# G's products with the weight blocks stationary and w2's 65 columns moving, G transposed afterwards

## The chip, the cores and the metric

The kernel runs on one core of a Trainium2 chip. The metric is the device time of one execution in microseconds (us), lower is better. Engines are called as in the profile: PE is TensorE (matmuls), PEld its weight loads, DVE is VectorE, ACT is ScalarE, POOL is GpSimd, SP is SyncE, which here only issues DMAs.

## The reference, cut to what matters

```python
def tok(idx, wte, w1, b1, w2, b2):       # idx (16, 1024)
    # x[t] = the embeddings (64 wide) of the last 16 tokens, side by side: 1024 columns
    h = tanh(x @ w1 + b1)                # (16, 1024, 64)
    return h @ w2 + b2                   # (16, 1024, 1024)
h = tok(...)
h = h + attn(layernorm(h))               # autocorrelation attention, general case
h = h + ffn(layernorm(h))
def ffn(x, W, bias, A, Bf, coeffs, scales):
    out = x @ W.T + bias
    xa  = einsum('bsd,erd->ebsr', x, A)  # 16 experts of rank 16
    return out + einsum('ebsr,eor,e->bso', xa, Bf, coeffs * scales)
```

Since the token stage is linear in its 64 hidden values (and a constant), the feed-forward part can be applied to w2 once: G = [w2c; b] (W^T + A^T diag(coeffs*scales) Bf), a matrix of 65 rows and 1024 columns, where w2c is w2 (and b2 as row 65) with its mean taken off. Every one of the 128 tiles of output is then a product with 64 rows of w2c and 64 rows of G, scaled and shifted per token, plus a few rank-one rows.

## The kernel before, in words

**Work.** 16 sequences of 1024 tokens, 8 tiles of 128 tokens each. A sequence goes through three stages in a software pipeline, written out by hand as `step(g, u, front, mid, back)`: front (gather the embeddings, transpose them, convolve with w1: `transpose_rows`, `conv_half`, then ACT's tanh), mid (transpose h, moments, variance, the scalings on POOL, split of h into a high and a low part: `transpose_h`, `moments_of`, `transpose_scaled`), back (the output tiles: `even_tile`, `odd_tile`, `four_rank_terms`, and `tile_out` on ACT and DVE). Step k does the front of sequence k, the mid of sequence k-1 and the back of sequence k-2. Every engine works its instructions off in the written order; semaphores tie them together.

**Where G is made.** G must be ready for the back part of step 2. It is built on PE in pieces put between other work: `weight_product(c, halves)` (L1026) for the eight 128-row blocks c of W^T, c = 0 before the steps, 1 to 3 in step 0, 4 to 7 in step 1; then `low_rank_products` (L1071) adds the rank-256 part and sets `g_done`. These are plain fp32 matmuls; the profile shows each as two passes, each with a weight load of its own. Block c of W^T lies in `wT_sb`, which is the memory of `h_all`: POOL's copy of h into `h_all` in step 1 (L454) therefore waits for `g_done`. The 65-column stationary side is `w2cT`, the moving side 512 columns of `wT_sb`; the result is the 65x1024 matrix G in the PSUM banks 0 and 1 of `o_ps`.

**What is done with G, all in step 1.** ACT rounds its 64 rows into `w_hi[64:128]` (L587) and its row 65 into `g_hi` (L588). DVE computes the remainders `w_lo[64:128]` and `g_lo` (`g_lo_halves`, L756 and L758). SP then copies the single rows `g_hi` (twice) and `g_lo` by DMA into `extra` rows 2, 4 and 3 (`row_in`, L319), and copies the eight rows of `extra` to three further partition groups (L351, `rows_in`). `four_rank_terms(0)` of step 2 waits for `rows_in`; the main products of step 2 (L1099) wait for `g_hi_set` and `g_lo_set`, and for the high and low parts of sequence 0 (`hi_kept`, `lo_kept`).

**The order in step 1.** PE: `transpose_rows`, `transpose_h`, product 4, moments, products 5 to 7, low rank, `conv_half(0)`, `transpose_scaled`, `conv_half(1)`. ACT: h parts, G's two copies, `keep_odd(0)` (L541), `take_tanh(0)` (L546), two copies of the scaled h (L610), L612, `keep_odd(1)`, `take_tanh(1)`. DVE: h remainders, `scale_h` (L820 and on, waits for POOL's `beta`), `g_lo_halves`, `add_shifts(0)` (L797), remainders of the scaled h (L907, `lo_kept`), `add_shifts(1)`. `conv_half(1)` waits for `add_shifts(0)`, since both halves use the one bank `conv_ps`.

Of the kernel before, what the change touches and what calls it, by code (L numbers as in the profile page):

```python
# [33 lines left out]
P = 128  # L34
NSEQ, T, L = 16, 1024, 1024
E = 64
# [5 lines left out]
KC = L // P  # L42
# [25 lines left out]
def tower_kernel(nc, ids, wte, w1, b1, w2, b2, wT, bias, aT, bfT, coeffs, scales,  # L68
                 ident, dft, idft, acf, lags, out, force_general=False):
    ctx = ExitStack()  # L70
    with ctx:
# [6 lines left out]
        def sem(name):  # L78
            return ctx.enter_context(nc.semaphore(name))
# [6 lines left out]
        ident_sb = sb("ident_sb", [P, P])  # L86
# [9 lines left out]
        w_hi = sb("w_hi", [P, L], F32R)  # L96
# [5 lines left out]
        bfT_sb = sb("bfT_sb", [P, 2, L])  # L102
# [38 lines left out]
        obuf = sb("obuf", [P, 4, 2, L])  # L141
# [14 lines left out]
        wT_sb = h_all[:, :].rearrange("p (c n) -> p c n", c=KC)  # L156
        w1_ld = obuf[:, 0, 0, :].rearrange("p (j n) -> p j n", j=J)
        w2cT = obuf[:, 0, 1, 0:KC * (E + 1)].rearrange("p (c n) -> p c n", c=KC)
        xa_sb = obuf[0:E + 1, 1, 0, 0:ER]
        xaT_sb = obuf[:, 1, 0, ER:ER + 2 * (E + 1)].rearrange("p (c n) -> p c n", c=2)  # L160
        er_ld = obuf[:, 1, 0, 512:516]
        xbar_rows = xT[0][0:KC, 0:P]

        b_hi, b_lo = w_hi[E:E + 1, :], w_lo[E:E + 1, :]
        bias_hi, bias_lo = u_hi[1][0:1, :], u_lo[1][0:1, :]
        g_hi, g_lo = u_hi[1][96:97, :], u_lo[1][96:97, :]
# [12 lines left out]
        o_ps = ps("o_ps", [P, 4, 512])  # L179
# [13 lines left out]
        def y_view(hh):  # L193

            return (mix_ps, sum_ps)[hh][:, 0:4 * (E + 3)].rearrange("p (j two n) -> p j two n", j=2, two=2)

        def in_pairs(rows):

# [28 lines left out]
        mom_kept = sem("mom_kept")  # L227
# [2 lines left out]
        xa_done = sem("xa_done")  # L230
        xa_kept = sem("xa_kept")
        g_done = sem("g_done")
        base_hi_set = sem("base_hi_set")
        base_lo_set = sem("base_lo_set")
        g_hi_set = sem("g_hi_set")
        g_lo_set = sem("g_lo_set")
        row0_in, rows_in = sem("row0_in"), sem("rows_in")
# [53 lines left out]
        def in_step(k, g, u):  # L291

            return isinstance(g, int) and 2 * g + u == k
# [190 lines left out]
        def _(act):  # L484
# [36 lines left out]
            def step(g, u, front, mid, back):  # L521
                a, b, c = 2 * g + u, 2 * g + u - 1, 2 * (g - 1) + u
# [13 lines left out]
                def keep_odd(hh):  # L536

                    act.wait_ge(conv_done, 2 * a + hh + 1)
                    ge(act, shifts_added, 2 * a + hh)
                    n = HALF - hh  # L540
                    nc.scalar.copy(odd[0:E, HALF * hh + 1:HALF * hh + 1 + n], conv_ps[E:P, 0:n]).then_inc(odd_kept, 1)  # L541
# [40 lines left out]
                    keep_h_hi(1)  # L582
                    keep_h_hi(2)
                if in_step(1, g, u):
                    act.wait_ge(row0_in, 16 * 5)
                    act.wait_ge(g_done, 1)
                    nc.scalar.copy(w_hi[E:P, :], o_ps[0:E, 0:2, :].rearrange("p a n -> p (a n)")).then_inc(g_hi_set, 1)  # L587
                    nc.scalar.copy(g_hi, o_ps[E:E + 1, 0:2, :].rearrange("p a n -> p (a n)")).then_inc(g_hi_set, 1)  # L588
                if front:
                    keep_odd(0)  # L590
                if mid and not front:
                    keep_h_hi(0)
                if back:
# [63 lines left out]
        def _(dve):  # L657
# [88 lines left out]
                nc.vector.tensor_tensor(w_lo[0:E + 1, :], w2c[:, :], w_hi[0:E + 1, :].bitcast(F32), ALU.subtract).then_inc(base_lo_set, 1)  # L746
                nc.vector.tensor_tensor(bias_lo, bias_row[:, :], bias_hi.bitcast(F32), ALU.subtract).then_inc(base_lo_set, 1)

            gw = o_ps[0:E, 0:2, :].rearrange("p a n -> p (a n)")
            gb = o_ps[E:E + 1, 0:2, :].rearrange("p a n -> p (a n)")  # L750

            def g_lo_halves():

                dve.wait_ge(row0_in, 16 * 5)
                dve.wait_ge(g_hi_set, 1)
                nc.vector.tensor_tensor(w_lo[E:P, :], gw, w_hi[E:P, :].bitcast(F32), ALU.subtract).then_inc(g_lo_set, 1)  # L756
                dve.wait_ge(g_hi_set, 2)
                nc.vector.tensor_tensor(g_lo, gb, g_hi.bitcast(F32), ALU.subtract).then_inc(g_lo_set, 1)  # L758
# [15 lines left out]
            def step(g, u, front, mid, back):  # L774
                a, b, c = 2 * g + u, 2 * g + u - 1, 2 * (g - 1) + u
# [18 lines left out]
                def add_shifts(hh):  # L794
                    dve.wait_ge(odd_kept, 2 * a + hh + 1)
                    cols = slice(HALF * hh, HALF * (hh + 1))
                    nc.vector.tensor_tensor(hT[u][E * hh:E * hh + E, 0:HALF], conv_ps[0:E, :], odd[0:E, cols],  # L797
                                            ALU.add).then_inc(shifts_added, 1)
# [82 lines left out]
                    keep_h_lo(1)  # L881
                if in_step(1, g, u):
                    scale_h()
                    g_lo_halves()
                if front:
                    add_shifts(0)
                if back:
                    tile_out(c, u, 4)
                if not front and not mid:
# [38 lines left out]
            with dve.If(need != 0):  # L928
# [6 lines left out]
                with dve.Fori(0, NSEQ * NT) as t:  # L935
# [67 lines left out]
                    for n in range(2):  # L1003
                        last = nc.vector.tensor_scalar(spec_w[:, P * n:P * (n + 1)], sum_ps[:, P * n:P * (n + 1)],
                                                       er_w[:, n:n + 1], None, ALU.mult)
# [9 lines left out]
        def _(pe):  # L1015
            mm, tr = nc.tensor.matmul, nc.tensor.transpose
# [4 lines left out]
            for c in range(KC):  # L1021
                bank = (sum_ps, mix_ps)[c // 4]
                last = tr(bank[:, (E + 1) * (c % 4):(E + 1) * (c % 4 + 1)], w2c[:, P * c:P * (c + 1)], ident_sb[0:E + 1, 0:E + 1])
            last.then_inc(w2T_done, 1)

            def weight_product(c, halves):  # L1026

                if c % 2 == 0:
                    pe.wait_ge(wT_in[c // 2], 16)
                for n in halves:  # L1030
                    mm(o_ps[0:E + 1, n, :], w2cT[:, c, :], wT_sb[:, c, 512 * n:512 * (n + 1)], start=(c == 0), stop=False)

            def xa_product(first, end):

# [6 lines left out]
            for c in range(KC):  # L1041
                last = mm(o_ps[0:E + 1, 2, 0:E + 1], w2cT[:, c, :], w2cT[:, c, :], start=(c == 0), stop=(c == KC - 1))
# [28 lines left out]
            def low_rank_products():  # L1071
                pe.wait_ge(bfT_in, 16)
                for e in range(2):
                    for n in range(2):
                        last = mm(o_ps[0:E + 1, n, :], xaT_sb[:, e, :], bfT_sb[:, e, 512 * n:512 * (n + 1)], start=False, stop=(e == 1))
                last.then_inc(g_done, 1)

            def xbar_correlation():

# [9 lines left out]
            def step(g, u, front, mid, back):  # L1089
                a, b, c = 2 * g + u, 2 * g + u - 1, 2 * (g - 1) + u  # L1090
# [43 lines left out]
                def transpose_scaled():  # L1134

                    pe.wait_ge(u_ready, b + 1)
                    for j in range(NT // 2):
                        last = tr(sum_ps[:, P * j:P * (j + 1)], bh_row[:, 2 * j:2 * j + 2, :].rearrange("p i e -> p (i e)"),  # L1138
                                  ident_sb[:, :])
                    last.then_inc(ut_done, 1)  # L1140
                    pe.wait_ge(x_ready, b + 1)
                    ge(pe, et_lo_kept, 2 * (a + front))
                    for q in range(NT // 2):
                        last = tr(et_ps[:, P * q:P * (q + 1)],  # L1144
                                  x_row[:, 2 * q:2 * q + 2, :, :].bitcast(F32).rearrange("p i d x -> p (i d x)"), ident_sb[:, :])
                    last.then_inc(xt_done, 1)
# [32 lines left out]
                def conv_half(hh):  # L1179

                    if in_step(0, g, u) and hh == 0:
                        pe.wait_ge(shift_set, 2)
                        pe.wait_ge(pads_set, 2)
                        pe.wait_ge(pad_conv_kept, 1)
                    if hh == 0:
                        pe.wait_ge(et_lo_kept, 2 * a + 2)
                    ge(pe, shifts_added, 2 * a + hh)
                    col = PAD + HALF * hh
                    for m in range(J // 2):
                        mm(conv_ps[:, :], shift_hi[:, 2 * m:2 * m + 2, :], et_hl[u][:, col - 2 * m:col - 2 * m + HALF],  # L1190
                           start=(m == 0), stop=False)
                    if hh == 0:
                        pe.wait_ge(et_top_kept, a + 1)
                        pe.wait_ge(et_back_kept, a + 1)
                    for m in range(J // 4):
                        last = mm(conv_ps[:, :], shift_lo[:, 2 * m:2 * m + 2, :], et_hh[u][:, col - 2 * m:col - 2 * m + HALF],  # L1196
                                  start=False, stop=(m == J // 4 - 1))
                    last.then_inc(conv_done, 1)
# [12 lines left out]
                if in_step(1, g, u):  # L1211
                    transpose_rows()
                    transpose_h()
                    weight_product(4, (0, 1))
                    moments_of(0)
                    moments_of(1)
                    for k in range(5, KC):
                        weight_product(k, (0, 1))
                    low_rank_products()
                    conv_half(0)  # L1220
                    transpose_scaled()
                    conv_half(1)
                    return
# [66 lines left out]
            with pe.If(need != 0):  # L1290
# [26 lines left out]
                with pe.Fori(0, NSEQ * NT) as t:  # L1317
# [30 lines left out]
                    for e in range(2):  # L1348
                        for c in range(KC):
                            last = mm(sum_ps[:, P * e:P * (e + 1)], aT_sb[:, c, P * e:P * (e + 1)], ab1[:, P * c:P * (c + 1)],  # L1350
                                      start=(c == 0), stop=(c == KC - 1))
# [53 lines left out]
```

## Time and profile before

| | |
|---|---|
| runs | 399.44, 400.08, 402.02 us; median 400.08 |
| profiled execution | 399.41 us, its span on the core 397.5 us |
| busy | PE 96%, DVE 70%, ACT 62%, POOL 54% |
| chain that ended last | PE 84%, POOL 6%, engines waiting for nothing shown 4%, DVE 2%, DMA 2% |
| granted TensorE clock | 0.996 in the mean |
| instructions | 6799 |

The span is the time from the first to the last instruction; the profiled execution's own time is 1.9 us longer. All times below are microseconds from the start of the span. Matmuls are pipelined: their records overlap, so the time that one costs is read from start to start of the ones in a row, not from its own duration.

### The profile page before, as it was taken

How to read it: one execution, taken by the hardware profiler on the slowest of the kernel's cores; microseconds unless marked ns; L12 is line 12 of the kernel's file. 1: busy time of each engine (PE TensorE's matmuls, PEld its weight loads, DVE VectorE, ACT ScalarE, POOL GpSimd, SP SyncE). 2: the span in 40 equal slices, each digit the busy share in tenths (PEclk: the TensorE clock that was granted, in tenths of full speed). 3: DMA queues.
4: the chain of work that ended last, by engine and by line, in shares of the span. 5: the costliest groups of instructions: out<-in, count | busy, mean ns of one | idle time of the engine just before them, and what ended most of it. 6: DMA issues, size and time to landing. Idle time of an engine off the chain costs nothing.

```text
span 397.5 us, 6799 instructions
## 1 busy us (share of the span) xinstructions
PE 380.2 (96%) x1908; PEld 276.5 (70%) x1908; DVE 276.3 (70%) x602; ACT 246.3 (62%) x362; POOL 214.7 (54%) x284
## 2 busy tenths in 40 slices
PE   1998999999999999999999999999999999999993
PEld 1554567777778777777777777777777777777662
DVE  2855567686868777786868687777868696876752
ACT  2524465766667666757666676667576666765642
POOL 6745748475574748374665747473846654312200
PEclk9999999999999999999999999999999999999998
DMA  9793045545545555555455455555554654445475
GB/s 213 216 353 112 12 130 213 187 192 206 209 174 211 192 221 224 211 202 207 172 212 223 157 208 205 221 224 202 200 215 166 223 213 155 203 195 240 194 307 215
DMA packets 28692, 79.86 MB, mean 201 GB/s; under 512 B 7194, under 2 KB 8490, under 8 KB 28676
## 3 DMA queue, kind: packets, MB, share of 16 engines
q1 hardware_dynamic: 23968, 75.19, 48.2%
q0 software_dynamic: 4096, 4.20, 5.3%
q10 hardware_dynamic: 612, 0.27, 0.4%
q8 instruction: 8, 0.13, 0.2%
q14 instruction: 8, 0.07, 0.0%
HBM read 12.40 MB, written 67.12 MB: 200 GB/s over the span
## 4 chain that ended last, share of the span: by engine, by line
PE 84%; POOL 6%; issue 4%; DVE 2%; DMA 2%; SPq 0%; POOLq 0%; DVEq 0%
PE o_ps L1099 46%; PE conv_ps L1190 13%; PE o_ps L1125 7%; PE conv_ps L1196 7%; POOL gathered L405 5%; PE sum_ps L1164 2%; PE sum_ps L1176 2%; PE mix_ps L1176 2%; PE sum_ps L1138 2%; PE et_ps L1144 2%; PE et_ps L1154 2%; DMA extra<-extra 1%; DVE obuf L718 1%; DMA ids_sb<-in_ids 1%; POOL inv_std L440 1%
## 5 line engine op out<-in xcount | busy, mean ns | idle before, releaser
L405 POOL DMA_INDIRECT gathered<-in_wte,idx_now x128 | 128.0, 1000 | 44.1 <-issue 34.3
L518 ACT ACTIVATE obuf<-o_ps,mean_sb,a_sb 128x512 f32<-128x512 f32 x128 | 99.7, 779 | 75.4 <-PE o_ps L1125 47.2
L718 DVE TENSOR_SCALAR obuf<-o_ps,a_sb,mean_sb 128x512 f32<-128x512 f32 x128 | 102.4, 809 | 58.5 <-PE o_ps L1099 33.0
L1099 PE MATMUL o_ps<-w_hi,u_hi 128*128 128x512 f32 x256 | 110.3, 431 | 0.0
L1099 PE MATMUL o_ps<-w_hi,u_lo 128*128 128x512 f32 x256 | 101.2, 395 | 0.0
L1099 PE MATMUL o_ps<-w_lo,u_hi 128*128 128x512 f32 x256 | 101.1, 395 | 0.0
L1190 PE MATMUL conv_ps<-et_hl,shift_hi 128*128 128x512 f32 x256 | 65.4, 397 | 0.8 <-DVE hT L797 0.8
L1099 PEld LDWEIGHTS o_ps<-w_hi,u_hi 128*128 128x128 f32 x256 | 48.1, 188 | 21.5 <-issue 12.6
L1190 PEld LDWEIGHTS conv_ps<-et_hl,shift_hi 128*128 128x128 f32 x256 | 48.1, 188 | 13.5 <-DVE hT L797 1.6
L1099 PEld LDWEIGHTS o_ps<-w_lo,u_hi 128*128 128x128 f32 x256 | 48.1, 188 | 11.6
L1099 PEld LDWEIGHTS o_ps<-w_hi,u_lo 128*128 128x128 f32 x256 | 48.3, 189 | 6.7
L436 POOL TENSOR_SCALAR var_eps<-var 128x8 f32<-128x8 f32 x16 | 3.2, 198 | 87.8 <-DVE var L847 87.8
L541 ACT COPY odd<-conv_ps 64x512 f32<-64x512 f32 (+1 forms) x32 | 18.7, 584 | 38.7 <-PE conv_ps L1196 38.7
L797 DVE TENSOR_TENSOR hT<-conv_ps,odd 64x512 f32<-64x512 f32 x32 | 21.9, 683 | 26.1 <-ACT odd L541 25.7
L1196 PE MATMUL conv_ps<-et_hh,shift_lo 128*128 128x512 f32 x128 | 35.0, 395 | 0.0
L1125 PE MATMUL o_ps<-extra,xT 8*128 8x512 f32 x256 | 32.3, 495 | 0.7 <-DMA extra<-extra 0.6
L440 POOL TENSOR_TENSOR inv_std<-var_eps,minus_half 128x8 f32<-128x8 f32 x16 | 27.9, 1746 | 2.3 <-POOL var_eps L436 1.8
L1125 PEld LDWEIGHTS o_ps<-extra,xT 8*128 8x128 f32 x256 | 12.3, 181 | 24.3 <-issue 23.3
L450 POOL TENSOR_TENSOR beta<-var_eps,minus_half 128x8 f32<-128x8 f32 x16 | 26.9, 1682 | 2.3 <-POOL var_eps L448 1.8
L1196 PEld LDWEIGHTS conv_ps<-et_hh,shift_lo 128*128 128x128 f32 x128 | 24.1, 189 | 5.6
L546 ACT ACTIVATE hT<-hT,b_col 64x512 f32<-64x512 f32 x32 | 22.9, 716 | 3.6 <-DVE hT L797 3.3
L787 DVE TENSOR_TENSOR et_hl<-et_ps,et_hl 64x512 fp32r<-64x512 f32 x32 | 22.1, 689 | 3.6 <-ACT et_hl L528 2.7
(133 smaller groups left out, 440.7 us busy)
## 6 DMA issues: line engine op xcount, KB each, us to landing
out<-obuf SPq DMA_DIRECT2D x127, 512.0 KB, 2.8
h_all<-in_wT SPq DMA_DIRECT2D x4, 1024.0 KB, 6.5
gathered<-in_wte,idx_now POOLq DMA_INDIRECT x128, 2.9
aT_sb<-in_aT SPq DMA_DIRECT2D x1, 1024.0 KB
bfT_sb<-in_bfT SPq DMA_DIRECT2D x1, 1024.0 KB, 12.2
obuf<-in_w SPq DMA_DIRECT2D x2, 256.0 KB, 7.3
lagged<-xbar_twice SPq DMA_DIRECT2D x1, 512.0 KB, 3.7
out<-obuf SPq DMA_DIRECT2D x2, 256.0 KB, 3.0
```

Source lines behind the costliest of these rows:

```text
L405: pool.indirect_dma_start(gathered[p][:, i, :], None, wte, bass.IndirectOffsetOnAxis(ap=idx_now[p][:, i:i + 1].bitcast(U32), axis=0),).the ...
L440: pool.tensor_tensor(inv_std[:, :], var_eps[:, :], minus_half[:, :], ALU.pow).then_inc(scal_step, 1)
L450: pool.tensor_tensor(beta[:, :], var2_eps[:, :], minus_half[:, :], ALU.pow).then_inc(scal_step, 1)
L518: nc.scalar.activation(obuf[:, q, i % 2, 0:512], o_ps[:, 2 * (i % 2), :], ACT.Identity, bias=mean_sb[pc][:, i:i + 1], scale=a_sb[pc][:, i: ...
L546: nc.scalar.activation(hT[u][rows, 0:HALF], hT[u][rows, 0:HALF], ACT.Tanh, bias=b1_col[rows, 0:1]).then_inc(tanh_done, 1)
L718: nc.vector.tensor_scalar(obuf[:, q, i % 2, 512:L], o_ps[:, 2 * (i % 2) + 1, :], a_sb[pc][:, i:i + 1], mean_sb[pc][:, i:i + 1], ALU.mult, ...
L787: nc.vector.tensor_tensor(lo, pair_bank(et_ps, odd_tiles), hi.bitcast(F32), ALU.subtract).then_inc(et_lo_kept, 1)
L797: nc.vector.tensor_tensor(hT[u][E * hh:E * hh + E, 0:HALF], conv_ps[0:E, :], odd[0:E, cols], ALU.add).then_inc(shifts_added, 1)
L1099: last = mm(o_ps[:, 2 * (i % 2) + n, :], lhsT, rhs[:, 512 * n:512 * (n + 1)], start=(i % 2 == 0 and f == 0), stop=(i % 2 == 1 and f == len ...
L1125: ins = mm(o_ps[:, k, :], xT[u][rows, P * q:P * (q + 1)], extra[rows, 512 * (k % 2):512 * (k % 2 + 1)], start=(k >= 2), stop=(k < 2))
L1190: mm(conv_ps[:, :], shift_hi[:, 2 * m:2 * m + 2, :], et_hl[u][:, col - 2 * m:col - 2 * m + HALF], start=(m == 0), stop=False)
L1196: last = mm(conv_ps[:, :], shift_lo[:, 2 * m:2 * m + 2, :], et_hh[u][:, col - 2 * m:col - 2 * m + HALF], start=False, stop=(m == J // 4 - 1))
```

## The change

The two sides of G's products change places. The stationary side is now a 128x128 block of `wT_sb` (or `bfT_sb`), the moving side `w2cT` (or `xaT_sb`) with its 65 columns: eight matmuls per block row c where there were two, ten block rows in all. The result is G transposed, in eight pieces of 128x65, four to a bank (`gT_bank`). ACT copies both banks to `gT_sb`; PE turns the eight pieces back (`turn_g`, after `conv_half(0)`) into the banks 2 and 3 of `o_ps`; ACT's and DVE's work on G reads them there. On ACT this work moves behind `keep_odd(0)`, on DVE `g_lo_halves` moves behind `add_shifts(0)`.

```diff
 # weight_product(c, halves), PE
-                for n in halves:
-                    mm(o_ps[0:E + 1, n, :], w2cT[:, c, :], wT_sb[:, c, 512 * n:512 * (n + 1)], start=(c == 0), stop=False)
+                for half in halves:
+                    for n in range(KC // 2):
+                        col = P * (KC // 2 * half + n)
+                        mm(gT_bank(half)[:, n, :], wT_sb[:, c, col:col + P], w2cT[:, c, :], start=(c == 0 and n == 0), stop=False)
 # low_rank_products, PE
-                    for n in range(2):
-                        last = mm(o_ps[0:E + 1, n, :], xaT_sb[:, e, :], bfT_sb[:, e, 512 * n:512 * (n + 1)], start=False, stop=(e == 1))
+                    for n in range(KC):
+                        last = mm(gT_bank(n // 4)[:, n % 4, :], bfT_sb[:, e, P * n:P * (n + 1)], xaT_sb[:, e, :], start=False, stop=(e == 1 and n % 4 == 3))
                 last.then_inc(g_done, 1)
+            def turn_g():
+                pe.wait_ge(gT_kept, 2)
+                pe.wait_ge(mom_kept, 5)
+                for n in range(KC):
+                    last = tr(o_ps[0:E + 1, 2 + n // 4, P * (n % 4):P * (n % 4 + 1)], gT_sb[:, n, :], ident_sb[:, :])
+                last.then_inc(g_turned, 1)
 # step 1, PE
                     low_rank_products()
                     conv_half(0)
+                    turn_g()
                     transpose_scaled()
                     conv_half(1)
 # step 1, ACT
                 if in_step(1, g, u):
-                    act.wait_ge(row0_in, 16 * 5)
                     act.wait_ge(g_done, 1)
-                    nc.scalar.copy(w_hi[E:P, :], o_ps[0:E, 0:2, :].rearrange("p a n -> p (a n)")).then_inc(g_hi_set, 1)
-                    nc.scalar.copy(g_hi, o_ps[E:E + 1, 0:2, :].rearrange("p a n -> p (a n)")).then_inc(g_hi_set, 1)
+                    for half in range(2):
+                        nc.scalar.copy(gT_sb[:, 4 * half:4 * half + 4, :], gT_bank(half)).then_inc(gT_kept, 1)
                 if front:
                     keep_odd(0)
+                if in_step(1, g, u):
+                    act.wait_ge(row0_in, 16 * 5)
+                    act.wait_ge(g_turned, 1)
+                    nc.scalar.copy(w_hi[E:P, :], o_ps[0:E, 2:4, :].rearrange("p a n -> p (a n)")).then_inc(g_hi_set, 1)
+                    nc.scalar.copy(g_hi, o_ps[E:E + 1, 2:4, :].rearrange("p a n -> p (a n)")).then_inc(g_hi_set, 1)
 # step 1, DVE
                 if in_step(1, g, u):
                     scale_h()
-                    g_lo_halves()
                 if front:
                     add_shifts(0)
+                if in_step(1, g, u):
+                    g_lo_halves()
```

## Rows read from the trace of the kernel before

**Rows 1.** Windows: start:end and length; PE, PEld, DVE, ACT, POOL busy; PEclk; DMA
```profile
54.00:385.00 331.00, 330.98 (x1700) 247.32 (x1699) 243.15 (x525) 221.63 (x327) 179.61 (x235) 1.00 0.53 205
...
391.40:394.50 3.10, 0.00 (x0) 0.00 (x0) 0.59 (x1) 0.56 (x1) 0.00 (x0) 1.00 0.86 329
394.60:397.50 2.90, 0.00 (x0) 0.00 (x0) 0.00 (x0) 0.00 (x0) 0.00 (x0) 0.50 0.04 12
```

**Rows 2.** The chain in order of time, 0 to 80: start, length, what
```profile
42.87 0.69 DVE u_rows L820
...
44.50 1.22 DVE w_lo L756
...
45.75 1.24 DVE u_lo L758
...
47.00 1.76 DMA extra<-u_lo
...
52.96 0.51 PE o_ps L1125 x4
```

**Rows 3.** PE's timeline, 28 to 51: start, length of the group, what
```profile
30.99 0.66 PE L1154 MATMUL et_ps<-ident_sb,gathered 128*128 128x128 f32 x4 [1.19 <-DMA gathered<-in_wte,idx_now]
...
34.55 5.31 PE L1031 MATMUL o_ps<-h_all,obuf 128*65 128x512 f32 x12
39.70 3.60 PE L1075 MATMUL o_ps<-bfT_sb,obuf 128*65 128x512 f32 x8
...
45.91 0.60 PE L1138 MATMUL sum_ps<-ident_sb,u_rows 128*128 128x128 f32 x4
46.35 0.60 PE L1144 MATMUL et_ps<-ident_sb,x_row 128*128 128x128 f32 x4
47.74 2.12 PE L1190 MATMUL conv_ps<-et_hl,shift_hi 128*128 128x512 f32 x8 [0.79 <-DVE hT L797]
...
50.74 0.47 PE L1099 MATMUL o_ps<-w_hi,u_hi 128*128 128x512 f32 x1
```

**Rows 4.** Timelines of PE and PEld: short fp32 operations before 35
```profile
33.64 0.62 PE L1176 MATMUL mix_ps<-moments_two,hT 128*128 128x134 f32 x4
34.09 0.62 PE L1176 MATMUL sum_ps<-moments_two,hT 128*128 128x134 f32 x4
...
13.71 0.29 PEld L1052 LDWEIGHTS o_ps<-moments,hbar 1*128 1x128 f32 x2
...
27.79 0.28 PE L1068 MATMUL mix_ps<-ident_sb,obuf 65*128 65x65 f32 x2
```

**Rows 5.** One line's instructions: durations ns min/median/max
```profile
L1176 PEld LDWEIGHTS mix_ps<-moments_two,hT x64: 190/190/192, 33.2 to 359.1; 128*128 128x128 f32 x64
...
L1052 PEld LDWEIGHTS o_ps<-moments,hbar x2: 181/182/184, 13.7 to 13.8; 1*128 1x128 f32 x2
...
L1068 PE MATMUL mix_ps<-ident_sb,obuf x2: 221/222/223, 27.8 to 27.9; 65*128 65x65 f32 x2
...
L1031 PE MATMUL o_ps<-h_all,obuf x32: 591/592/1057, 11.1 to 39.3; 128*65 128x512 f32 x32
```

**Rows 6.** ACT's timeline
```profile
8.84 0.37 ACT L498 COPY obuf<-mix_ps 128x260 f32<-128x260 f32 x1
...
43.39 1.01 ACT L587 CAST w_hi<-o_ps 64x1024 fp32r<-64x1024 f32 x1 [6.92 <-PE o_ps L1075]
...
46.11 0.58 ACT L541 COPY odd<-conv_ps 64x512 f32<-64x512 f32 x1 [0.69 <-PE conv_ps L1196]
...
48.47 1.19 ACT L610 CAST u_hi<-sum_ps 64x512 fp32r<-64x512 f32 x2
```

**Rows 7.** DVE's and POOL's timelines
```profile
47.01 0.68 DVE L797 TENSOR_TENSOR hT<-conv_ps,odd 64x512 f32<-64x512 f32 x1
49.08 1.41 DVE L907 TENSOR_TENSOR u_lo<-sum_ps,u_hi 64x512 fp32r<-64x512 f32 x2 [1.39 <-ACT u_hi L610]
...
37.38 0.20 POOL L436 TENSOR_SCALAR var_eps<-var 128x8 f32<-128x8 f32 x1
```

More of the change, by code:

```diff
@@ L162, in tower_kernel @@
         xbar_rows = xT[0][0:KC, 0:P]
+        gT_sb = obuf[:, 2, 0, 0:KC * (E + 1)].rearrange("p (n e) -> p n e", n=KC)
         b_hi, b_lo = w_hi[E:E + 1, :], w_lo[E:E + 1, :]
@@ L195, in y_view, with gT_bank @@
             return (mix_ps, sum_ps)[hh][:, 0:4 * (E + 3)].rearrange("p (j two n) -> p j two n", j=2, two=2)
+        def gT_bank(half):
+            return o_ps[:, half, 0:KC // 2 * (E + 1)].rearrange("p (n e) -> p n e", e=E + 1)
         def in_pairs(rows):
@@ L232, in tower_kernel @@
         g_done = sem("g_done")
+        gT_kept = sem("gT_kept")
+        g_turned = sem("g_turned")
         base_hi_set = sem("base_hi_set")
@@ L747, in base_lo_halves @@
                 nc.vector.tensor_tensor(bias_lo, bias_row[:, :], bias_hi.bitcast(F32), ALU.subtract).then_inc(base_lo_set, 1)
-            gw = o_ps[0:E, 0:2, :].rearrange("p a n -> p (a n)")
-            gb = o_ps[E:E + 1, 0:2, :].rearrange("p a n -> p (a n)")
+            gw = o_ps[0:E, 2:4, :].rearrange("p a n -> p (a n)")
+            gb = o_ps[E:E + 1, 2:4, :].rearrange("p a n -> p (a n)")
             def g_lo_halves():
```

## The prediction

> **What bounds the kernel now.** I read the windows first: from 54 to 385 PE is busy 330.98 of 331.00 us [rows 1]. Nothing behind the start-up has room, so whatever PE gains or loses before 54 shifts the rest rigidly. The change only touches what comes before, so the next views are the chain in order of time and the timelines up to 54. The chain leaves `scale_h` (DVE, 42.87) for the two remainders of G (44.50 and 45.75, done at 46.99), the DMA of row `g_lo` (47.00), the copies of `extra`, and reaches PE's `four_rank_terms(0)` at 52.96 [rows 2]. From then on PE never stops. So the question is one date: when do G's rows reach `extra`? PE's own stream before it is nearly as tight: an idle 1.19 in front of 30.99 (gathered rows, from POOL) and 0.79 in front of 47.74 (`add_shifts(0)`, which DVE starts at 47.01 behind G's remainders) [rows 3, 7].
>
> **The products themselves.** Before, a pass of 512 columns costs (39.70 - 34.55)/12 = 0.429 us [rows 3]; a block row is 4 passes, 1.72. After, it is 8 matmuls of 2 passes, 16 passes with a 128-column weight load and 65 moving columns. The trace has no such pass, so I bound it. The moving side alone: `xa_by_columns` streams 65 columns, its two passes start 0.28 - 0.22 = 0.06 us apart [rows 4, 5]. The load alone: two 128-column fp32 loads in front of 3-column matmuls start 0.29 - 0.18 = 0.108 apart, so they are the limit there [rows 4, 5]. Do load and stream add up? In the moments each pass has a 128-column load of 190 ns and streams 134 columns, and passes start (34.09 - 33.64)/4 = 0.113 apart [rows 4, 5]: the load lies wholly beside the stream before it. So the pass costs the larger of the two, 0.109 (the load, nearest row 0.108; 0.113 at the upper end). The ends for the range are 0.060 and 0.108 + 0.060 = 0.168. A block row is then 16 x 0.109 = 1.74 against 1.72: **nothing is gained**, since the halved stream makes the doubled load the limit.
>
> The Trainium skill says the opposite of overlap: in "TensorE: Matmul & The Clock Gate", the section "Measured speedup vs the span model", a weight load overlaps a running matmul only where the row group differs, and here all 128 rows are used. By that rule the pass would be the sum of both; the moments' rows contradict it, and I give it a small chance below.
>
> Products 0 to 3 lie before 30.99: 64 passes, at most 0.3 us more, under the 1.19 us that PE waits there for gathered rows; without that cover they would cost 0.3. Product 4 and the two 0.11 passes of the moments do not move POOL: its `var_eps` at 37.38 starts with no idle before it, behind a gather [rows 7]. After 30.99 come six block rows: 96 x 0.109 - 24 x 0.429 = +0.15 us. `g_done` gates POOL's copy into `h_all` and five gathers, all +0.15, and sequence 2's rows are needed after `four_rank_terms(0)`, which moves more.
>
> **The way of G after them.** Before, ACT's copy into `w_hi` starts at 43.39 right behind the products and ends at 44.40, just as DVE leaves `scale_h` (0.69 from 42.87, then small ones to about 44.43), and the remainders start at 44.50 [rows 2, 6]. After:
> - ACT copies the two banks, 0.37 each [rows 6], from about 43.5 to 44.2, in time it waited away before; PE is in `conv_half(0)`. Cost nothing; without that cover 0.7.
> - `conv_half(0)` ends at 45.91 [rows 3] + 0.15 = 46.06. `turn_g` is 8 fp32 transposes at (46.35 - 45.91)/4 = 0.11 [rows 3] = 0.87: to 46.93, result at about 47.10 (a transpose group's record of 0.60 is 0.16 longer than its 0.44 of starts).
> - ACT has ended `keep_odd(0)` (0.58 from 46.11 + 0.15) at 46.84 and waits for `g_turned`: `w_hi` 47.19 to 48.20, `g_hi` to 49.2 (1.01 each) [rows 6]. SP's two DMAs of `g_hi` follow at once, beside DVE's work.
> - DVE has added shifts at 46.9 to 47.6, in the gap. The remainders start at 48.24 instead of 44.50 and end after the same 2.49 at 50.73. The last row's DMA starts at 50.74, and the rest, the row, SP's three copies and their landing, takes 52.96 - 47.00 = 5.96 as before [rows 2]: **56.70 instead of 52.96, +3.74 us**.
>
> Beside it: PE's `transpose_scaled` moves to 46.93 to 47.80; `conv_half(1)` starts at 47.8 without its wait of 0.79, thus when it did before (47.74). The 0.87 of `turn_g` is paid by that idle time. Queued behind ACT's later copies are `take_tanh(0)` and L610: L610 (before at 48.47) now starts at 49.2 + 0.75 = 49.9, so DVE's L907, 1.41 from 49.08, now runs from about 50.7 behind the remainders to 52.1 [rows 6, 7]. The main products of `even_tile(0)`, before at 50.74 [rows 3], wait for it until 52.15, are six passes of 512 columns, at about 0.24 each 1.4 (the eight of L1190 span 2.12 with their tail [rows 3]), and end at 53.55. That wait of 1.4 is inside the longer one: PE then stands 3.15 until 56.70. `keep_odd(1)`, `add_shifts(1)`, `take_tanh(1)` end near 53.8 and are needed at 57. Sum: 399.41 (profiled) + 3.74 = 403.15; against the median 400.08, 0.67 above the profiled one, 403.8. I say 403.7.
>
> **The rivals.**
> - *The clock falls in the new gap.* PE would stand 1.4, work 1.4, stand 3.15. After the last matmul of the trace PE does nothing from 391.40; the granted clock is 1.00 to 394.50 and 0.50 after 394.60 [rows 1]: 3.1 us of nothing were survived there, a bit more was not. Idle stretches of 1.2 cost nothing. If it falls to 1.2 GHz, the first pass of 512 columns in the trace shows what that means: 1057 ns against 592 [rows 5]. How long it would stay low no row says (at the start it was low up to that pass at 11.1); if about as long as the gap, 3 us of work run at half speed and cost 1.5 more: 405.2. For: the gap is as long as the one survived. Against: work of 1.4 us in front.
> - *Load and stream add up* (by the skill's rule above): 0.168 per pass, 96 x 0.059 = 5.7 more after 30.99, and 64 x 0.059 = 3.8 before less the cover of 1.19, 2.6: 412. The point from which it decides is any pass above 0.12. Against it stand the moments.
> - *Not slower: the load is hidden better than its row says*, pass 0.060. Then `g_done` comes 96 x 0.049 = 4.7 earlier. But `scale_h` still waits for POOL's `beta` and ends at 44.43; the new order puts `add_shifts(0)` (0.68 [rows 7]) in front, so the remainders start at 45.15 instead of 44.50: +0.65, 400.7. Below a pass of about 0.077 this limit holds, and no pass makes the time better than before. For: only that loads of half the width took 0.06; against: the 0.108.
> - *Faster by over 1%* needs G's rows at 49, which neither `scale_h` nor the 5.96 of DMAs permits; I leave it for what I may have overlooked.
>
> **How the numbers follow.** A measurement of this kernel tells some 1%, 4 us, from no change. Forecast (+3.7, from +3.2 to +4.9 with a pass of 0.113 and the noise of the runs): 0.70. Clock: 0.10. Adding up: 0.06. Short passes: 0.11. Faster: 0.03. The range 402.0 to 406.0 holds the forecast and the clock case, 0.80. The limit of 1% is at 404.08, just above the forecast: a quarter to a third of its 0.70 lies beyond (0.22), with clock 0.10 and adding 0.06, 0.38 slower; 0.59 within 1%; 0.03 faster. The sign is surer than that: an increase has 0.95.
>
> **What would show it.** The new products at 0.109 from start to start, `g_done` near 43.5; `turn_g` at 46.1; the `w_hi` copy at 47.2; the remainders at 48.2; PE idle before the main products of step 2 and about 3 us before the first L1125 group at 56.7, then none; clock 1.00 throughout. Products at 0.06, or an L1125 group before 55, would make it wrong, as would later idle time on PE that absorbs the shift.

## The result, and the profile after

The changed kernel takes 406.57 us (median of 4, 405.43 to 406.83) against 399.76 (median of 4, 399.06 to 402.02): ratio 1.0164, 95% interval 1.0138 to 1.019, **6.8 us slower**. The forecast was 403.7, range 402.0 to 406.0: right in sign, too small, outside the range. The profiled execution took 406.65, its span is 404.8, 7.3 longer than before.

PE's timeline after, from the first products to step 2; columns as in [rows 3]. L1057 is the first product of w2c with itself, which starts the stretch; L1052 are the products with A^T (aT below), L1177 the transposes of gathered rows, L1046 are G's products, L1090 the low-rank ones, L1098 `turn_g`, L1148 `four_rank_terms`:

```profile
9.35 2.02 PE L1057 MATMUL o_ps<-obuf 128*65 128x65 f32 x16 [1.20 <-ACT obuf L506]
...
11.16 1.92 PE L1046 MATMUL o_ps<-obuf,h_all 128*128 128x65 f32 x8
12.88 0.32 PE L1063 MATMUL o_ps<-hbar,moments 65*65 65x1 f32 x2
...
15.94 3.56 PE L1052 MATMUL sum_ps<-aT_sb,obuf 128*65 128x256 f32 x8
...
19.63 0.66 PE L1177 MATMUL et_ps<-ident_sb,gathered 128*128 128x128 f32 x4
20.12 1.89 PE L1052 MATMUL sum_ps<-aT_sb,obuf 128*65 128x256 f32 x8
...
32.98 0.60 PE L1177 MATMUL et_ps<-ident_sb,gathered 128*128 128x128 f32 x4
...
36.58 5.47 PE L1046 MATMUL o_ps<-obuf,h_all 128*128 128x65 f32 x48
41.88 3.74 PE L1090 MATMUL o_ps<-obuf,bfT_sb 128*128 128x65 f32 x32
45.43 2.10 PE L1213 MATMUL conv_ps<-et_hl,shift_hi 128*128 128x512 f32 x8
47.36 1.09 PE L1219 MATMUL conv_ps<-et_hh,shift_lo 128*128 128x512 f32 x4
48.30 1.04 PE L1098 MATMUL o_ps<-ident_sb,obuf 128*65 128x128 f32 x8
...
54.73 0.47 PE L1122 MATMUL o_ps<-w_hi,u_hi 128*128 128x512 f32 x1 [1.74 <-DVE u_lo L920]
...
58.67 0.51 PE L1148 MATMUL o_ps<-extra,xT 8*128 8x512 f32 x4 [2.29 <-DMA extra<-extra]
```

The same stretch of the kernel before, ahead of [rows 3]; L1042, L1037 and L1154 there are L1057, L1052 and L1177 here:

```profile
9.26 2.02 PE L1042 MATMUL o_ps<-obuf 128*65 128x65 f32 x16 [1.23 <-ACT obuf L498]
...
14.38 1.94 PE L1037 MATMUL sum_ps<-aT_sb,obuf 128*65 128x256 f32 x8
...
16.46 0.66 PE L1154 MATMUL et_ps<-ident_sb,gathered 128*128 128x128 f32 x4
```

Three things are to be seen, against these and [rows 2, 3]:
- The new products cost what was forecast: (41.88 - 36.58)/48 = 0.110 us a pass.
- But PE is late before any of it matters. The first group of L1052 takes 3.56, the second, eight passes too, 1.89: TensorE is still at its lower level of 1.2 GHz at 16 us. (The windows of this profile print a granted clock of 1.00 for this stretch too; at the start of a profile the level is therefore read from the durations.) Before, the first such group already took 1.94: the higher level, 2.4 GHz. So a group is slow that the change doesn't touch. PE reaches the gathered rows of sequence 0 at 19.63 instead of 16.46 and those of sequence 1 at 32.98 instead of 30.99, without waiting for them: the cover of 1.19 is used up and 1.99 is lost.
- From `turn_g` on the forecast's distances hold within 0.3 (48.30 to L1148 is 10.37; forecast 46.06 to 56.70, 10.64), with both predicted idle stretches (1.74 and 2.29; forecast 1.4 and 3.15). Between 32.98 and 48.30 PE loses 0.40 where the forecast had 0.15, so two small misses cancel.

The windows of the same profile (columns as in [rows 1]) show the rest:

```profile
36.60:45.40 8.80, 8.80 (x82) 8.80 (x80) 5.50 (x21) 1.77 (x3) 5.61 (x8) 1.00 0.05 10
...
56.38:58.66 2.28, 0.00 (x1) 0.00 (x0) 0.00 (x0) 0.00 (x0) 0.14 (x1) 1.00 0.26 45
...
60.30:63.60 3.30, 3.30 (x12) 2.72 (x11) 1.12 (x5) 1.43 (x4) 0.00 (x0) 0.50 0.39 159
63.70:400.00 336.30, 334.50 (x1711) 248.77 (x1710) 246.01 (x530) 222.60 (x327) 179.24 (x234) 1.00 0.54 207
```

After the two idle stretches the granted clock is 0.50 from 60.3 to 63.7, with PE busy all the time: the work of 1.7 us at 2.4 GHz is done there in 3.4. So 7.3 = 5.71 (L1148 at 58.67 instead of 52.96) + 1.6, and 5.71 = 3.74 forecast + 1.97.

G's way on ACT, and then on DVE, in the timelines of the changed kernel, the rows that answer [rows 2, 6, 7]:

```profile
49.43 1.01 ACT L601 CAST w_hi<-o_ps 64x1024 fp32r<-64x1024 f32 x1 [0.35 <-PE o_ps L1098]
```
```profile
49.11 0.68 DVE L809 TENSOR_TENSOR hT<-conv_ps,odd 64x512 f32<-64x512 f32 x1 [3.82 <-ACT odd L549]
50.53 1.22 DVE L768 TENSOR_TENSOR w_lo<-o_ps,w_hi 64x1024 fp32r<-64x1024 f32 x1 [0.74 <-ACT w_hi L601]
51.78 1.22 DVE L770 TENSOR_TENSOR u_lo<-o_ps,u_hi 1x1024 fp32r<-1x1024 f32 x1
53.04 1.41 DVE L920 TENSOR_TENSOR u_lo<-sum_ps,u_hi 64x512 fp32r<-64x512 f32 x2
```

`add_shifts(0)` (L809) stands first, `w_hi` starts 1.13 after `turn_g`, the remainders follow it, and `lo_kept` (L920) comes last at 54.45, which PE's main products wait for: each in the order and at the distances of the forecast.

### The profile page after: what moved, and what is told of

It is laid out like the page before. It is cut to its first block, busy times and chain, and to the rows that moved or that the text cites. A ratio compares the mean times of both kernels' runs of the same rounds, so it can differ in the third digit from the quotient of the medians.

```text
span 404.8 us, 7058 instructions
## 1 busy us (share of the span) xinstructions
PE 385.9 (95%) x2036; PEld 293.5 (73%) x2036; DVE 276.0 (68%) x602; ACT 246.9 (61%) x364; POOL 213.4 (53%) x284
## 4 chain that ended last, share of the span: by engine, by line
PE 93%; DMA 2%; DVE 2%; ACT 0%; ACTq 0%; SPq 0%; issue 0%; DVEq 0%
PE o_ps L1122 46%; PE conv_ps L1213 14%; PE conv_ps L1219 7%; PE o_ps L1148 7%; PE o_ps L1046 4%; PE sum_ps L1187 2%; PE sum_ps L1199 2%; PE mix_ps L1199 2%; PE et_ps L1177 2%; PE sum_ps L1161 2%; PE et_ps L1167 2%; DMA b_col<-in_b 1%; PE sum_ps L1052 1%; PE o_ps L1090 1%; DMA extra<-extra 1%; DVE obuf L730 1%
## 5 line engine op out<-in xcount | busy, mean ns | idle before, releaser
L809 DVE TENSOR_TENSOR hT<-conv_ps,odd 64x512 f32<-64x512 f32 x32 | 21.9, 683 | 29.5 <-ACT odd L549 29.0
L1148 PE MATMUL o_ps<-extra,xT 8*128 8x512 f32 x256 | 32.2, 495 | 2.4 <-DMA extra<-extra 2.3
L1148 PEld LDWEIGHTS o_ps<-extra,xT 8*128 8x128 f32 x256 | 12.3, 181 | 26.0 <-issue 23.2
## 6 DMA issues: line engine op xcount, KB each, us to landing
bfT_sb<-in_bfT SPq DMA_DIRECT2D x1, 1024.0 KB, 12.9
```

What stands on the lines that cost most here:

```text
L1148: ins = mm(o_ps[:, k, :], xT[u][rows, P * q:P * (q + 1)], extra[rows, 512 * (k % 2):512 * (k % 2 + 1)], start=(k >= 2), stop=(k < 2))
```

## The experiments

**Two ways to take the clock out.** Theory: 3.7 us are G's longer way, 2.0 the late rise of the clock, the rest its fall in the gap. Rival: the form of the products, or a fourth cause, costs 2 us or more at full clock too. Warm-up:

```diff
+            pe.wait_ge(warm_set, 1)          # DVE has set hT[0] to 1.0
+            for n in range(3):
+                mm(conv_ps[:, :], hT[0][:, 0:P], hT[0][:, 0:HALF], start=True, stop=True)
             pe.wait_ge(consts_in, 16)
 ...
             last.then_inc(w2T_done, 1)
+            mm(conv_ps[:, :], hT[0][:, 0:P], hT[0][:, 0:HALF], start=True, stop=True)
```

Fill (7 before the main products' wait, 9 before `rows_in`):

```diff
+                for n in range(7):           # and 9 before pe.wait_ge(rows_in, 48)
+                    mm(mix_ps[:, :], shift_hi[:, 0:2, :], et_hl[1][:, PAD:PAD + HALF], start=True, stop=True)
```

> The kernel before, with four extra fp32 matmuls of 512 columns on a constant tile (three before PE's first transposes, one between them and the first products), so that TensorE works from about 1.5 us on. Clock theory (start-up level matters only where PE is late): the granted clock is up before 9 us, products 0 start at the higher level, but the kernel before waits 1.19 us for gathered rows at 30.99 anyway, so L1125 still starts within 0.3 of 52.96 and the time is 399.8 give or take 0.6. Rival (the start-up's PE time is on the path in the kernel before too): 1 us or more faster.

Measured 399.07 (10 runs, 398.6 to 401.31) against 399.48: ratio 1.0002 (0.9982 to 1.0021). The clock theory holds for the time, but not by the wait that was expected. PE's timeline:

```profile
14.44 1.94 PE L1043 MATMUL sum_ps<-aT_sb,obuf 128*65 128x256 f32 x8 [1.28 <-DMA aT_sb<-in_aT]
...
29.67 0.60 PE L1160 MATMUL et_ps<-ident_sb,gathered 128*128 128x128 f32 x4
...
47.47 2.12 PE L1196 MATMUL conv_ps<-et_hl,shift_hi 128*128 128x512 f32 x8 [1.81 <-DVE hT L799]
```

The gathered rows are there at 29.67 in this execution, and PE doesn't wait for them: the cover of 1.19 is not the same in every execution. PE is done with `transpose_scaled` early and waits 1.81 instead of 0.79 for `add_shifts(0)`; L1131 starts at 52.71.

> The changed kernel with the same four extra matmuls. Clock theory: of the 5.7 us by which G's rows came late, 2.0 come from TensorE being at the lower level until 19.3; with it up by 9 us the products before 31 us are done in time, PE waits for gathered rows again, turn_g starts near 46.1 and the first L1148 group near 56.7, and the time is 403.5 (405.2 if the clock falls again in the gap after). Rival (the products themselves or something else of the change is dearer by 2 us before 33 us, at full clock too): turn_g stays at 48.3 and L1148 at 58.7, time 405.0 to 406.6.

Measured 404.73 (4 runs, 403.55 to 405.37): ratio 1.0135 (1.0114 to 1.0157), between the two theories. The profile is of the fastest of the four, 403.55; the others have mean granted clocks of 0.987 to 0.991 against its 0.991. PE's timeline, warm-up in front (L1036), then the windows:

```profile
1.45 4.58 PE L1036 MATMUL conv_ps<-hT 128*128 128x512 f32 x6 [1.45 <-DVE hT L671]
...
9.27 1.16 PE L1063 MATMUL o_ps<-obuf 128*65 128x65 f32 x16 [0.58 <-ACT obuf L507]
10.26 1.06 PE L1052 MATMUL o_ps<-obuf,h_all 128*128 128x65 f32 x8
12.32 0.28 PE L1069 MATMUL o_ps<-hbar,moments 65*65 65x1 f32 x2 [1.00 <-DVE moments L694]
...
17.42 1.11 PE L1183 MATMUL et_ps<-ident_sb,gathered 128*128 128x128 f32 x4
...
57.05 0.51 PE L1154 MATMUL o_ps<-extra,xT 8*128 8x512 f32 x4 [2.32 <-DMA extra<-extra]
```
```profile
8.50:11.90 3.40, 2.24 (x25) 1.92 (x24) 1.21 (x8) 1.95 (x5) 2.68 (x3) 1.00 1.21 241
12.00:15.30 3.30, 2.87 (x20) 2.37 (x21) 2.77 (x10) 1.60 (x2) 2.42 (x5) 0.99 0.58 178
15.40:18.70 3.30, 3.30 (x12) 2.02 (x11) 2.09 (x4) 0.28 (x2) 2.69 (x3) 0.51 0.80 248
```

The clock was up, and **fell again** from 15.4 to 18.6, behind block 0 of the new products, an idle 1.00 in the middle of it and the small matmuls after it. In the kernel before with the same warm-up it did not, over the same stretch and with an idle 1.28 in it. So in this profile the warm start didn't last through the new block 0, and this run can't isolate the 2.0. L1154 came at 57.05, and no fall followed although PE stood 1.71 and 2.32 before it.

> The changed kernel with 7 and 9 extra fp32r matmuls of 512 columns in PE's two idle stretches of step 2 (before the main products wait, and before L1148 waits for the copied rows), writing a free bank. Clock theory: no fall of the clock at 60.3; L1148 still at 58.7 or as late as the start-up makes it; PE without idle time from then; 405.0, that is 1.5 less than the changed kernel in the runs in which its clock fell and the same in the others. Rival (the clock's fall costs nothing that PE has not lost already): no change, 406.5.

Measured 405.69 (405.52 to 408.57): ratio 1.0178 (1.0138 to 1.0218). No fall in the profile: PE is back at 58.98 and the span is 403.6, 1.2 under the profiled changed kernel's 404.8. The medians (405.69 and 406.57) don't separate it from the changed kernel.

> Both of these in the changed kernel. Clock theory: only the forecast's term is left, the later way of G's rows: L1148 near 56.7, no low clock from 9 us to the end of PE's work, 3.7 above the kernel before, 403.5. Rival (there is a fourth cause): above 404.5.

Measured 405.39, from 402.21 to 406.97: inconclusive. Its four runs have mean granted clocks of 0.989, 0.998, 0.993 and 0.983, and their times are in that order: 402.21 at 0.998, 406.97 at 0.983. In the profile the clock was low from 12.9 to 19.6.

**Block 0 alone, both ways round.** Since the warm-up couldn't hold the clock, the form of block 0 itself was changed.

```diff
 # old0_after: in the changed kernel, G's first block left out
+                    if c == 0:
+                        mm(o_ps[0:E + 1, half, :], w2cT[:, c, :], wT_sb[:, c, 512 * half:512 * (half + 1)], start=True, stop=True)
+                        continue
 # new0_before: in the kernel before, G's first block left out
+                    if c == 0:
+                        for n in range(KC // 2):
+                            col = P * (KC // 2 * half + n)
+                            mm(o_ps[:, half, (E + 1) * n:(E + 1) * (n + 1)], wT_sb[:, c, col:col + P], w2cT[:, c, :],
+                               start=(n == 0), stop=(n == 3))
+                        continue
```

> The changed kernel with block 0 of the products (the two halves before the steps) in the old form, G's first block left out of the sum. Form theory (at the lower clock level the new form, loads with a half as long stream behind each, does not bring the clock up as the old one does): the clock rises near 12 to 16 instead of 19 to 20, PE reaches 19.6 some 2 to 3 us earlier, turn_g near 46.2, L1148 near 56.8, time 403.7 (1.6 more if the clock falls in the gap). Rival (the late rise is chance of the executions, or comes from anything else in the start-up): rise at 19 to 20, L1148 at 58.7, 405.5 to 406.6.

Measured 403.55 (403.0 to 404.32): ratio 1.0096 (1.0073 to 1.012). The form theory holds. The profile is of the slowest of the four.

```profile
9.57 2.02 PE L1060 MATMUL o_ps<-obuf 128*65 128x65 f32 x16 [1.17 <-ACT obuf L506]
...
14.73 1.89 PE L1055 MATMUL sum_ps<-aT_sb,obuf 128*65 128x256 f32 x8
...
16.93 0.66 PE L1180 MATMUL et_ps<-ident_sb,gathered 128*128 128x128 f32 x4
...
56.24 0.51 PE L1151 MATMUL o_ps<-extra,xT 8*128 8x512 f32 x4 [2.61 <-DMA extra<-extra]
```

This is PE's timeline. The first aT group (L1055) takes 1.89, thus at the higher level, and PE is at the gathered rows of sequence 0 at 16.93. Seven blocks and the low-rank part in the new form, the turn and the order cost 56.24 - 52.96 = 3.3 here. In the median 3.0 of the 6.8 us go with block 0's new form.

> The reverse: the kernel before with block 0 of the products in the new form (its result overwritten by block 1, so G lacks its first block). Form theory: clock up at 19 to 20 instead of 12.25, PE 3 us later at 20, 1.2 of it absorbed in front of the gathered rows at 31, the rest on G's way: L1125 near 54.8, time 401.5. Rival: unchanged, 399.5.

Measured 403.33 (402.49 to 404.9): ratio 1.0089 (1.0065 to 1.0112), more than expected. Of the profile, PE's timeline:

```profile
12.29 2.02 PE L1049 MATMUL o_ps<-obuf 128*65 128x65 f32 x16 [4.46 <-ACT obuf L498]
...
18.88 3.62 PE L1044 MATMUL sum_ps<-aT_sb,obuf 128*65 128x256 f32 x8
...
22.72 1.11 PE L1161 MATMUL et_ps<-ident_sb,gathered 128*128 128x128 f32 x4
```

Here the first product also started 3 us late, at 12.29, behind ACT; that differs from execution to execution (9.2 to 9.7 in ten of the profiles, 11.3 to 12.4 in four). What ACT waits for is the DMA of b1. Its timeline here, and then in the kernel before:

```profile
11.39 0.31 ACT L495 ACTIVATE hbar<-b_col 64x128 f32<-64x128 f32 x1 [3.37 <-DMA b_col<-in_b]
```
```profile
8.37 0.31 ACT L495 ACTIVATE hbar<-b_col 64x128 f32<-64x128 f32 x1 [1.69 <-DMA b_col<-in_b]
```

This tanh of b1 stands ahead of ACT's copies of the transposed w2 (L498), and it starts at 10.4 to 11.6 in the four late profiles, at 8.3 to 8.8 in the ten others. The form's share is therefore read from the first product to the gathered rows' transposes: 22.72 - 12.29 = 10.43, against 16.46 - 9.26 = 7.2 in the kernel before. All profiles fall in two groups: block 0 old 7.1, 7.2, 7.2 (one of them warmed), 7.4, 7.7, 8.1 and 8.3; block 0 new and not warmed 10.3, 10.4, 10.4, 10.4 and, with 16 columns in the later blocks, 10.0. That is 1.7 to 3.3 us for block 0 alone. (Warmed, the new form has 8.2 and 9.0.) Why the other three runs, at 402.49 to 403.61, also lie above the expected 401.5 is not shown.

**The order and the turn.**

```diff
 # order_before: in the kernel before
+                if front:
+                    keep_odd(0)              # ACT: now ahead of G's two copies
                     act.wait_ge(g_done, 1)
 ...
                     scale_h()
-                    g_lo_halves()
                 if front:
                     add_shifts(0)
+                if in_step(1, g, u):
+                    g_lo_halves()
```

> The kernel before with only the changed kernel's order: ACT rounds G behind keep_odd(0), DVE takes G's remainders behind add_shifts(0). Products, their form and their place stay, nothing is transposed. Order theory (most of the forecast's 3.74 is the order, not the transposes): ACT's w_hi at 46.75, remainders from 47.8 instead of 44.5, L1125 at 56.2, 3.3 more than before: 402.8, and up to 1.7 more where the clock falls in PE's gap. Rival (the turn behind conv_half(0) is what costs): 1 us at most, 400.5.

Measured 404.13 (403.64 to 407.46): ratio 1.0122 (1.01 to 1.0145). With no product and no transpose changed, the order alone costs 4.7 us in the median. Its profile started late (11.36), so the distance is read, on PE's timeline, from the end of `conv_half(0)` (start of L1139, or of `turn_g` in the changed kernel) to `four_rank_terms(0)`:

```profile
47.57 0.60 PE L1139 MATMUL sum_ps<-ident_sb,u_rows 128*128 128x128 f32 x4
...
53.65 0.47 PE L1100 MATMUL o_ps<-w_hi,u_hi 128*128 128x512 f32 x1 [1.49 <-DVE u_lo L908]
...
57.99 0.80 PE L1126 MATMUL o_ps<-extra,xT 8*128 8x512 f32 x4 [2.69 <-DMA extra<-extra]
```

10.42 here, 58.67 - 48.30 = 10.37 in the changed kernel, 52.96 - 45.91 = 7.05 in the kernel before [rows 2, 3]: the order alone brings the whole 3.3, and the turn, which runs beside `keep_odd(0)`, adds nothing to it. The window behind the gap:

```profile
57.80:64.50 6.70, 6.51 (x25) 5.49 (x26) 2.15 (x6) 2.85 (x5) 0.00 (x0) 0.50 0.19 78
```

Gaps of the same size (1.49 and 2.69) are followed by a fall of the clock here too, and for 6.8 us, with the products in the old form: the fall doesn't need the new products. Of the four profiles with unfilled gaps three show it (this one, the changed kernel, old0_after), warm_after doesn't; of the three with filled gaps none does. So the gap makes a fall there possible, not certain. This profile is of the slowest of five runs; four of the five have mean clocks of 0.988 to 0.991, so much of the 1.3 us over the expected 402.8 may be such falls; late starts are the other candidate.

> The changed kernel with turn_g right behind the low-rank products, and ACT's and DVE's work on G before keep_odd(0) and add_shifts(0), as in the kernel before. With a start-up as late as the changed kernel's: products end at 45.4, turn at 46.3 to 47.2, remainders from 48.4 instead of 50.5, L1148 near 56.7 instead of 58.7, PE's gap before it near 1 us instead of 2.3, so no fall of the clock there: 403.5. If the way of G were not what sets L1148: 406.5.

```diff
                     low_rank_products()
+                    turn_g()
                     conv_half(0)
-                    turn_g()
 # and on ACT and DVE G's work stands before keep_odd(0) and add_shifts(0) again
```

Measured 404.4 (403.61 to 405.68): ratio 1.0133 (1.0106 to 1.016), 2.2 under the changed kernel. L1147 starts at 57.09 with 0.38 idle instead of 2.29 and no fall follows, though the first aT group is as late (3.62) as in the changed kernel. As expected but for 0.9 in the median.

Both edits, this one and old0_after's, in one kernel:

> The changed kernel with both repairs: block 0 in the old form (left out of the sum) and turn_g right behind the low-rank products with ACT's and DVE's old order. If the two causes add: clock up by 12 to 16, turn_g at 43.7, remainders from 45.8, L1148 near 54.2, 401.1, that is 1.2 us above the kernel before, the way through the copy and the transposes alone. If they don't add (another wait takes over): 402.5 or more.

Measured 401.59 (6 runs, 400.54 to 404.44): ratio 1.0047 (1.002 to 1.0074). The causes add: the two edits alone took 3.0 and 2.2 off 406.57, together 5.0. Its profile is of the slowest run, which started late (12.44), and in which the clock was low from 46.4 to 49.7, behind the new products and the 0.74 that PE waits for ACT's copy of G transposed.

And the fill in old0_after:

> The changed kernel with block 0 in the old form and the 16 extra matmuls in PE's two gaps of step 2. Clock theory: no low clock from 16 us to the end of PE's work; only the forecast's term is left: L1150 near 56.4, 3.6 above the kernel before, 403.1, and never the 1.5 that the clock's fall added in one profile of the kernel without the fill. Rival: same times as without the fill, falls included.

Measured 403.39 (402.93 to 404.56): ratio 1.0106 (1.0082 to 1.0131). In the profile the clock holds, L1153 is at 56.44 and the execution took 402.95: the forecast's term without clock effects, 403.1 expected. Against old0_after's 403.55 the medians show no difference. Its profiled run, the slowest of four at 404.32, has a mean clock of 0.991 and the low stretch; the others have 0.994 and 0.995, which suggests that they didn't have it.

**The limit of a pass.**

> The changed kernel with 16 moving columns instead of 65 in blocks 1 to 7 and the low-rank products (G's other columns left out). If the 128-column weight load is the limit of a pass: passes start 0.108 to 0.111 us apart as with 65 columns. If load and stream add: 0.07 to 0.12 less than with 65, if the stream were the limit: 0.03. A second question: whether the clock holds in the 8.8 us of such products from 36 us on, which it did with 65 columns; a fall there would double them to 0.215.

```diff
-                        mm(gT_bank(half)[:, n, :], wT_sb[:, c, col:col + P], w2cT[:, c, :], ...)
+                        w = E + 1 if c == 0 else WM          # WM = 16
+                        mm(gT_bank(half)[:, n, 0:w], wT_sb[:, c, col:col + P], w2cT[:, c, 0:w], ...)
```

One run, 414.96. PE's timeline and the windows of its step 1:

```profile
33.93 1.86 PE L1048 MATMUL o_ps<-obuf,h_all 128*128 128x16 f32 x16
35.64 0.70 PE L1201 MATMUL mix_ps<-moments_two,hT 128*128 128x134 f32 x4
...
36.63 7.67 PE L1048 MATMUL o_ps<-obuf,h_all 128*128 128x16 f32 x48
44.14 6.99 PE L1092 MATMUL o_ps<-obuf,bfT_sb 128*128 128x16 f32 x32
```
```profile
36.60:39.40 2.80, 2.80 (x28) 2.80 (x26) 2.73 (x12) 1.83 (x3) 1.21 (x3) 1.00 0.11 26
39.50:56.50 17.00, 17.00 (x69) 15.74 (x70) 2.72 (x10) 0.68 (x3) 8.34 (x11) 0.50 0.03 7
```

A pass with 16 columns costs (35.64 - 33.93)/16 = 0.107, with 65 it costs 0.110: the stream is not the limit, and load and stream do not add up. That it is the load, and not a fixed cost of each pass, the first lines of warm_after show: there L1063 streams 65 columns behind loads of 65, at the higher level, and its passes start (10.26 - 9.27)/16 = 0.062 apart. And the clock falls at 39.5 in the middle of the 16-column products, with PE and PEld busy without a break; with 65 columns it held through 8.8 us of them. Why it fell is open, and so is whether it would in another execution: this is one run.

**A version faster than both.** [Rows 2] put `g_lo` last on the way to `extra`. It needs only G's row 65, so that row goes first:

```diff
-                    nc.scalar.copy(w_hi[E:P, :], o_ps[0:E, 0:2, :]...).then_inc(g_hi_set, 1)
                     nc.scalar.copy(g_hi, o_ps[E:E + 1, 0:2, :]...).then_inc(g_hi_set, 1)
+                    nc.scalar.copy(w_hi[E:P, :], o_ps[0:E, 0:2, :]...).then_inc(g_hi_set, 1)
 # the same on DVE; SP waits for g_hi_set 1 and g_lo_set 1
```

> The kernel before with G's row 65 taken before its 64 rows on ACT and DVE, so that the DMAs into extra start 1.25 us earlier, at 45.75. If the rows' way alone sets L1125: it starts at 52.4, right behind the main products, 0.6 us earlier, and the time is 398.9 against 399.5. If PE's stream is as late anyway: no change.

Measured 398.8 (12 runs, 398.62 to 399.94) against 399.44 (19 runs): ratio 0.9984 (0.9973 to 0.9995), as expected: 0.6 us, small, but the interval excludes 1. PE's timeline:

```profile
52.16 0.51 PE L1125 MATMUL o_ps<-extra,xT 8*128 8x512 f32 x4
```

The idle 0.59 in front of L1125 is gone; PE stands 0.21 behind it instead, for ACT's tanh.

## Why the prediction was wrong

- **The products, 0.109 us a pass: right.** 0.110 measured, and the 16-column run, with the 0.062 of 65-column loads, shows the load as the limit. The rule of the Trainium skill that I weighed, that a load overlaps a running matmul only where the row group differs, stands in "TensorE: Matmul & The Clock Gate" in the section "The mechanism", not where I placed it. The runs contradict it for this case: 0.110 a pass, not 0.168, so a full-row load lies beside the matmul before it. They fit another sentence of that section, by which a load into the background weight buffer is pulled ahead too. Two slips didn't matter: 96 x 0.109 - 24 x 0.429 is 0.17, not 0.15, and the two passes of `xa_by_columns`, 0.06 apart, have loads of 128 columns and 65 rows (L1068), not of half the width; they are transposes, whose loads have records of 140 ns against the moments' 190, so their 0.06 bounds no plain product's load.
- **G's way, +3.74: right.** Without the start-up's share L1151 stands at 56.24 and L1153 at 56.44 (forecast 56.70), the times are 403.55 and 403.39 (forecast 403.7). The telling was incomplete: I spoke of `turn_g` and its result at 47.1, but `order_before` shows that the order alone brings as much (10.42 against 10.37 from the end of `conv_half(0)`), while early_after, with the old order, takes 1.8 more than the kernel before from the start of the low-rank products to `four_rank_terms(0)` (57.09 - 42.06 against 52.96 - 39.70): the copy and the transposes are not free where the order doesn't hide them. `add_shifts(0)` waits for `keep_odd(0)` and thus for all of `conv_half(0)`; whatever DVE has behind it can't start before 47.4.
- **The failed step: "Products 0 to 3 lie before 30.99: 64 passes, at most 0.3 us more, under the 1.19 us that PE waits there for gathered rows."** It priced all of them at the higher clock level, and put what block 0 does to the level behind it at nothing. Measured: PE 3.2 late at the first gathered rows, half of it from block 0 (aT products at 15.94 instead of 14.38), half from the first group of aT products, which the change doesn't touch (3.56 instead of 1.94); 1.99 is left after the cover of 1.19. [Rows 5] had the sign of it, a first pass of 1057 ns against 592, and I used it for the gap only. Block 0 in the old form brings the level up during or soon after it; in the new form, with the same engine busy without a break, the level stays low until the aT products. old0_after (rise back, 3.0 us less in the median) and new0_before (rise late in the kernel before) show it from both sides.
- **The clock in the gap: right in mechanism, its chance too low.** It had 0.10 and a price of 1.5; the profiled run paid 1.6, `order_before`'s about 3.1 (its span is 8.1 longer than the kernel before's, `four_rank_terms(0)` 5.0 later). The mean clocks of the other three runs (0.995, the profiled one 0.992) suggest that these did not pay it, so for the median of 406.57 it is not the main part. The median is 1 us over 399.76 + 3.7 + 2.0 = 405.5. This too goes with block 0's new form (old0_after's median is 403.55), but how it divides between a later rise, falls of the clock and late starts is open; no run separates them.
- The rivals of short passes (400.7) and of adding up (412) are both ruled out by the 0.110 a pass.
- The range was too narrow because it took the late G as a fixed sum and gave the clock one place only, the gap; the start-up at the lower level was a second place, outside all cases.

## What to carry to other kernels

Making the wide operand stationary and the narrow one moving moves the cost of an fp32 matmul from the stream to the weight load; price it by the load (0.107 to 0.110 us for 128 columns here), and expect no gain where the old stream was as long. Ask of each stretch that changes form not only how long it takes, but at which clock level it runs and whether it was what raised the level: a cover of idle time further on must be set against the stretch at its slow price. Before blaming a new operation for a later wait, look for the order: one step moved behind another engine's long chain cost the whole 3.3 us here that looked like the price of the transposes.

## What the runs showed of the hardware

- With 128-column loads and 16 moving columns PE and PEld were busy all the time, and in the one run the granted clock fell from 1.00 to 0.50 at 39.5 and stayed there for 17 us; it rose at 56.5, behind convolutions of 512 columns that ran from 50.97. With 65 columns it held for 8.8 us at the higher level in the changed kernel, but during such products it did not rise from the lower one at the start, in five profiles of five without a warm-up.
- A warm-up of four matmuls gained nothing in the kernel before (1.0002), and in the changed kernel's profile the level was lost again at 15.4.
- Full-height fp32 weight loads ran beside the matmul before them: passes start 0.107 us apart with 16 moving columns, 0.110 with 65, 0.113 with 134 (128-column loads), and 0.062 with 65-column loads and 65 moving columns, all at 2.4 GHz. At 1.2 GHz a pass of the new form took 0.215 ((12.88 - 11.16)/8, L1046 and L1063 of the changed kernel).
- The first product starts at 9.2 to 9.7 us in ten profiles and at 11.3 to 12.4 in four. In all fourteen ACT's tanh of b1 comes right before, released by the DMA of b1: it starts at 8.3 to 8.8 in the ten and at 10.4 to 11.6 in the four. A start later than the slack at 31 us is passed on: order_before, with the products of the kernel before, started 2.1 late and reached the gathered rows at 32.62 without a wait. Why this DMA lands late in some executions was not looked into.
